# Expert stage of a convolution and attention hybrid: other group steps, two routing products, half precision pairs

## The reference

```python
def _L1_ffn_ref(x, router_w, router_b, expert_w, expert_b):
    B, N, D, C, E, K = (8, 8192, 128, 128, 8, 2)
    router_probs = jax.nn.softmax(x @ router_w + router_b, axis=-1)
    top_p, top_i = jax.lax.top_k(router_probs, K)
    top_p = top_p / jnp.sum(top_p, axis=-1, keepdims=True)
    expert_out = jnp.einsum('bnd,edc->bnec', x, expert_w) + expert_b
    gathered = jnp.take_along_axis(expert_out, top_i[..., None], axis=2)
    return jnp.einsum('bnk,bnkc->bnc', top_p, gathered)

t = t + _L1_ffn_ref(_ln_t(t), ...)      # residual, _ln_t is a layer norm per token
```

## Time and profile before

| | us |
|---|---|
| median of 3 runs | 2772.21 (2766.97 to 2772.77) |
| the profiled execution, its own time | 2768.08 |
| its span in the profile | 2766.2 |
| start of the expert stage in it | 2392.07 |
| first `scaled`, first `scaled_halves` (tile 0) | 2425.17, 2426.4 |
| last `scaled_halves` (tile 127) | 2760.47 |

### The profile page before, as it was taken

One profiled execution on the slowest core, in us unless ns is written; L12 is line 12 of the kernel. 1 busy time (PEld: TensorE's weight loads), 2 busy tenths in 40 slices (PEclk: granted clock), 3 DMA queues, 4 the chain that ended last, 5 costly groups with the idle time before them and its releaser, 6 DMA issues. The chain is left out here.

```text
span 2766.2 us, 33616 instructions
## 1 busy us (share of the span) xinstructions
PE 2267.1 (82%) x10862; PEld 1298.3 (47%) x10862; DVE 2087.2 (75%) x3702; ACT 1668.3 (60%) x2322; POOL 563.4 (20%) x693
## 2 busy tenths in 40 slices
PE   0594646759860599999999999999999999778877
PEld 0581213657630344444444444444444444466665
DVE  5327879756598778888888888888888888655566
ACT  0113012642237378888888888888888888556655
POOL 0002240002106502201221022101200000036567
PEclk9997866555565699999999999999999999779989
DMA  4600213000004000000000000000000000000001
GB/s 149 221 22 1 121 37 85 0 8 1 1 1 121 5 1 1 1 1 1 1 1 1 1 1 1 1 1 1 1 1 1 1 1 1 8 12 27 24 23 39
DMA packets 81022, 64.09 MB, mean 23 GB/s; under 512 B 11475, under 2 KB 78931, under 8 KB 79332
## 3 DMA queue, kind: packets, MB, share of 16 engines
q1 hardware_dynamic: 73604, 60.21, 6.6%
q10 hardware_dynamic: 7264, 1.94, 0.4%
HBM read 36.91 MB, written 25.17 MB: 22 GB/s over the span
## 5 line engine op out<-in xcount | busy, mean ns | idle before, releaser
L1751 ACT ACTIVATE inner<-banks,key_bias,scales 128x1024 f32<-128x1024 f32 x512 | 616.9, 1205 | 211.4 <-PE banks L1624 206.3
L1873 DVE TENSOR_TENSOR weights_low<-weights,weights_high 128x1024 f16<-128x1024 f32 x512 | 675.3, 1319 | 17.0
L1758 ACT ACTIVATE weights<-inner 128x1024 f32<-128x1024 f32 x512 | 541.1, 1057 | 16.1 <-DVE weights_low L1873 0.3
L1869 DVE CAST weights_high<-weights 128x1024 f16<-128x1024 f32 x512 | 371.0, 725 | 180.7 <-ACT weights L1758 167.6
L1624 PE MATMUL banks<-queries_high,keys_high 128*128 128x512 f16 x1024 | 304.6, 379 | 0.7 <-ACT inner L1751 0.7
L1639 PE MATMUL banks<-weights_high,tokens_low 128*128 128x512 f16 x1024 | 304.6, 379 | 0.0
L1624 PE MATMUL banks<-queries_low,keys_high 128*128 128x512 f16 x1024 | 304.6, 379 | 0.0
L1639 PE MATMUL banks<-weights_low,tokens_high 128*128 128x512 f16 x1024 | 304.6, 379 | 0.0
L1624 PE MATMUL banks<-queries_high,keys_low 128*128 128x512 f16 x1024 | 304.6, 379 | 0.0
L1639 PE MATMUL banks<-weights_high,tokens_high 128*128 128x512 f16 x1024 | 304.5, 379 | 0.0
L1947 POOL CAST sums_high<-sums 128x512 f16<-128x512 f32 x32 | 39.4, 1231 | 1089.6 <-ACT sums L1741 1071.7
(11 more groups left out here) (439 smaller groups left out, 3863.8 us busy)
## 6 DMA issues: line engine op xcount, KB each, us to landing
images_a<-in_x SPq DMA_DIRECT2D x4, 2048.0 KB, 16.8
tokens_scratch<-images_a SPq DMA_DIRECT2D x4, 2048.0 KB, 13.1
images_b<-tokens_scratch SPq DMA_DIRECT2D x32, 256.0 KB, 2.8
mixed_scratch<-images_a SPq DMA_DIRECT2D x4, 2048.0 KB, 13.1
spare<-in_x SPq DMA_DIRECT2D x32, 256.0 KB, 2.8
result<-group_result SPq DMA_DIRECT2D x32, 256.0 KB, 2.3
images_b<-mixed_scratch SPq DMA_DIRECT2D x10, 768.0 KB, 5.0
table<-tables ACTq DMA_DIRECT2D x1, 805.5 KB, 14.6
```

The costliest lines, as they stand in the source:

```text
L1751: act.activation(m.inner[:, t % 2, :], m.pair[t % 2], ACT.Exp, scale=m.fs[:, 1:2], bias=m.kb[:, c // QN % 2, k:k + 1]).then_inc(s.inner, 1)
L1758: act.activation(m.wt[:, t % 2, :], m.inner[:, t % 2, :], ACT.Exp).then_inc(s.outer, 1)
L1869: vec.tensor_copy(m.wH[:, t % DEEP, :], m.wt[:, t % 2, :]).then_inc(s.high, 1)
L1873: vec.tensor_tensor(m.wL[:, t % DEEP, :], m.wt[:, t % 2, :], m.wH[:, t % DEEP, :], ALU.subtract)\
```

## The change

`stage_ffn`, its plan and its buffers are changed, and nothing else:

- Types: tokens and weights are split into pairs of float16 instead of float32r. To fit the range, the weights are divided by a size (root of the sum of squares of all weights) and multiplied by 2^15. This is computed at the stage's start: a reduction of squares on DVE, one matmul with ones on PE, a floor on DVE, a root on ACT, a reciprocal and two scalings on DVE. The logits are multiplied back (`down`), and the gates' divisor gets `up`.
- Routing: `w8H` has eight more columns, the low parts of the routing weights, so the high tokens meet 16 columns in one matmul and the low tokens 8 in another. Eight matmuls for each group replace twelve. DVE adds the two halves where it copied the logits before. The logits of all batches use one place in PSUM, with a new wait (`copied`) at a batch's first group.
- Order: `normed` stands behind `scaled`, two tiles in the round of `prep` and two in the round after; `m.ln` has four buffers. `turn` and `high` stand two rounds later, `low` three, `logit` five (`DELAY`).
- Plan: batches of 3, 5, 8, 8, 8 groups. Groups begin in rounds 0, 0, 1, 1, 2, then 12 to 19 one in each, then 32, 34, 36, 39, 41, 43, 46, 48, and the same plus 32. The pieces of `algebra` stand in rounds 9 and 10 (four steps each), then from 27, 57 and 89 in four rounds with two steps each, where seven rounds had one step each.

```diff
-        m.w8H = sb(l2, "expert_weights_high", [P, EXPERTS * D + EXPERTS], F32R)[:, :]
-        m.w8L = sb(l2, "expert_weights_low", [P, EXPERTS * D + EXPERTS], F32R)[:, :]
-        m.ln = sb(l2, "normed", [P, 2, GRP, D])
-        m.lnH = sb(l2, "normed_high", [P, RING, GRP, P], F32R)
-        m.lnL = sb(l2, "normed_low", [P, RING, GRP, P], F32R)
+        m.w8H = sb(l2, "expert_weights_high", [P, EXPERTS * D + 2 * EXPERTS], F16)[:, :]
+        m.w8L = sb(l2, "expert_weights_low", [P, EXPERTS * D], F16)[:, :]
+        m.ln = sb(l2, "normed", [P, 4, GRP, D])
+        m.lnH = sb(l2, "normed_high", [P, RING, GRP, P], F16)
+        m.lnL = sb(l2, "normed_low", [P, RING, GRP, P], F16)
...
-BATCHES = [4, 8, 8, 8, 4]
-SETTLE = 11
+BATCHES = [3, 5, 8, 8, 8]
+DELAY = 5
...
         at, slots = first[k - 1] * GRP, BATCHES[k - 1] * GRP
+        parts = min(7, slots // 5)
+        spread = slots - 1 - parts - DELAY - 1
         for i in range(BATCHES[k]):
-            prep.setdefault(at + i * (slots - SETTLE) // BATCHES[k], []).append(first[k] + i)
-        for i in range(7):
-            pieces[at + slots - 8 + i] = k
-        exps[at + slots - 6] = k
+            prep.setdefault(at + i * spread // BATCHES[k], []).append(first[k] + i)
+        for i in range(parts):
+            pieces[at + slots - 1 - parts + i] = (k, parts)
+        exps[at + slots - parts] = k
...
-                reached(pe, s.gates, k - 1)
+                if t == first[k]:
+                    reached(pe, s.copied, k)
                 for j in range(GRP):
...
                     pe.matmul(part, m.lnH[:, t % RING, j, :], m.w8H[:, cols], start=True, stop=False)
-                    pe.matmul(part, m.lnH[:, t % RING, j, :], m.w8L[:, cols], start=False, stop=False)
-                    mm = pe.matmul(part, m.lnL[:, t % RING, j, :], m.w8H[:, cols], start=False, stop=True)
+                    mm = pe.matmul(part[:, 0:EXPERTS], m.lnL[:, t % RING, j, :], m.w8H[:, cols][:, 0:EXPERTS],
+                                   start=False, stop=True)
...
+            turn(0)
+            pe.wait_ge(s.cleared, 2)
+            pe.wait_ge(s.squared, 1)
+            pe.matmul(m.ps[7][:, 0:1], m.full, m.wsize[:, 0:1], start=True, stop=True).then_inc(s.summed, 1)
+            turn(1)
             for t in range(BATCHES[0]):
-                turn(t)
-                if t >= 1:
-                    logit(t - 1)
-            logit(BATCHES[0] - 1)
+                if t >= 2:
+                    turn(t)
+                logit(t)
             for n in range(NI):
                 expert(n)
+                for t in prep.get(n - DELAY, []):
+                    logit(t)
                 for t in prep.get(n - 2, []):
-                    logit(t)
-                for t in prep.get(n, []):
                     turn(t)
...
             for n in range(NI):
-                for t in prep.get(n, []):
-                    normed(t)
                 scaled(n)
                 for t in prep.get(n - 1, []):
+                    normed(t, (2, 3))
+                for t in prep.get(n - 2, []):
                     high(t)
+                for t in prep.get(n, []):
+                    normed(t, (0, 1))
...
-                c.step(vec.tensor_copy(logit, logits(k)))
+                wide = logits(k)
+                c.step(vec.tensor_scalar(logit, wide[:, :, 0], down, None, ALU.mult))
+                vec.scalar_tensor_tensor(out=logit, in0=wide[:, :, 1], scalar=down, in1=logit, op0=ALU.mult, op1=ALU.add)\
+                    .then_inc(s.copied, 1)
+                vec.wait_ge(s.copied, k + 1)
...
+                c.step(vec.tensor_scalar(total, total, up, None, ALU.mult))
...
-            c.step(vec.tensor_copy(m.w8H, m.w8))
-            vec.tensor_tensor(m.w8L, m.w8, m.w8H, ALU.subtract).then_inc(s.weights, 1)
-            for t in range(BATCHES[0]):
+            vec.tensor_tensor_reduce(square, m.w8, m.w8, 1.0, 0.0, ALU.mult, ALU.add, m.wsize[:, 0:1]).then_inc(s.squared, 1)
+            vec.wait_ge(s.summed, 1)
+            vec.tensor_scalar(m.wsize[:, 1:2], m.ps[7][:, 0:1], 1e-30, None, ALU.max).then_inc(s.floored, 1)
+            low(0)
+            vec.wait_ge(s.sized, 1)
+            c.step(vec.reciprocal(m.wsize[:, 3:4], m.wsize[:, 2:3]))
+            vec.tensor_scalar(down, m.wsize[:, 2:3], 2.0 ** -15, None, ALU.mult)
+            c.step(vec.tensor_scalar(up, m.wsize[:, 3:4], 2.0 ** 15, None, ALU.mult))
+            c.step(vec.tensor_scalar(m.w8H[:, 0:EXPERTS * D + EXPERTS], m.w8, up, None, ALU.mult))
+            vec.scalar_tensor_tensor(out=m.w8H[:, EXPERTS * D + EXPERTS:], in0=m.w8[:, EXPERTS * D:], scalar=up,
+                                     in1=m.w8H[:, EXPERTS * D:EXPERTS * D + EXPERTS], op0=ALU.mult, op1=ALU.subtract)\
+                .then_inc(s.weights, 1)
+            vec.scalar_tensor_tensor(out=m.w8L, in0=m.w8[:, 0:EXPERTS * D], scalar=up, in1=m.w8H[:, 0:EXPERTS * D],
+                                     op0=ALU.mult, op1=ALU.subtract).then_inc(s.weights, 1)
+            for t in range(1, BATCHES[0]):
                 low(t)
...
                 if n in pieces:
-                    work = work or algebra(pieces[n])
-                    next(work, None)
+                    k, parts = pieces[n]
+                    work = work or algebra(k)
+                    for _ in range(-(-8 // parts)):
+                        next(work, None)
...
-                for t in prep.get(n - 1, []):
+                for t in prep.get(n - 3, []):
                     low(t)
```

More of the change, by code:

```diff
@@ L311, in memory @@
         m.rank = sb(l2, "first_ranks", [P, EXPERTS])[:, :]
+        m.full = sb(l2, "ones_for_sums", [P, P])[:, :]
+        m.wsize = sb(l2, "weight_sizes", [P, 8])
     return m
@@ L1990, in batch_plan @@
         at, slots = first[k - 1] * GRP, BATCHES[k - 1] * GRP
+        parts = min(7, slots // 5)
+        spread = slots - 1 - parts - DELAY - 1
         for i in range(BATCHES[k]):
[L1992 to L1995 removed]
+            prep.setdefault(at + i * spread // BATCHES[k], []).append(first[k] + i)
+        for i in range(parts):
+            pieces[at + slots - 1 - parts + i] = (k, parts)
+        exps[at + slots - parts] = k
     return first, prep, pieces, exps
 def stage_ffn(nc, held, m, ins, out):
[L2002 removed]
+    s = semaphores(nc, held, "ffn", "loaded cleared biased v factor rooted weights ones normed turned high low logits shifted exp copied gates squared summed floored sized "
                    "tile_d tile_a chain scaled halved paired result stored0 stored1")
@@ L2090, in _, with normed @@
         def _(act):
-            def normed(t):
-                reached(act, s.turned, t - 1)
-                if t < 2:
+            def normed(t, tiles):
+                reached(act, s.turned, t - 3)
+                if t < 4:
                     act.wait_ge(s.ones, 1)
-                for j in range(GRP):
+                for j in tiles:
                     img = t * GRP + j
-                    e = act.activation(m.ln[:, t % 2, j, 0:D - 1], m.b[:, img, 0:D - 1], ACT.Identity,
+                    e = act.activation(m.ln[:, t % 4, j, 0:D - 1], m.b[:, img, 0:D - 1], ACT.Identity,
                                        scale=m.fac[:, 1, img:img + 1], bias=m.fac[:, 2, img:img + 1])
-                e.then_inc(s.normed, 1)
+                if tiles[-1] == GRP - 1:
+                    e.then_inc(s.normed, 1)
             def high(t):
@@ L2125, in _ @@
             for t in range(BATCHES[0]):
-                normed(t)
+                normed(t, range(GRP))
                 if t >= 1:
                     high(t - 1)
+                if t == 1:
+                    act.wait_ge(s.floored, 1)
+                    act.activation(m.wsize[:, 2:3], m.wsize[:, 1:2], ACT.Sqrt).then_inc(s.sized, 1)
             high(BATCHES[0] - 1)
```

20 lines of the change are left out of this document (10 added, 10 removed).

## The result

| | before | after |
|---|---|---|
| median, us | 2771.09 (4 runs, 2766.97 to 2772.77) | 2709.32 (4 runs, 2705.52 to 2712.36) |
| ratio, 95% interval | | 0.9779 (0.9762 to 0.9796) |
| profiled execution, its span | 2768.08, 2766.2 | 2705.52, 2703.7 |
| first `scaled`, first `scaled_halves` | 2425.17, 2426.4 | 2419.68, 2420.90 |
| last `scaled_halves` | 2760.47 | 2697.92 |

The change takes 62 us away. The windows of the changed kernel's last stage show where it ends up. Each runs from the start of `scaled_halves` of one tile to that of another (0, 12, 32, 64, 96, 127); the columns are those of the earlier trace rows.

What follows compares the result with a forecast made beforehand. Bound by engines waiting for each other, PE's list the chain with a hole. Terms from 2422 sum to 2708, plus 10 is span 2718, 48 less than 2766.2; 2772 - 48 = 2724 us, range 2700 to 2755.

Steps and rivals of the forecast that it cites:

- the allowance: 10 us added to the summed list for what it doesn't show: rounds at the lower clock and new small holes.
- tiles 0 to 8: Loop's first tiles, five groups begun: 24 us with PE at full clock from round 5, 31 if never; 28 taken.
- tiles 12 to 31: Eight group rounds 26.2, five quiet 7.7, four with a table 18.2, one 1.5: together 53.6 us.
- Rival 2: The lists run clean, no allowance, first tiles warm: 2710 us, or 2705 with ACT evening out its rounds; chance 0.13.
- The hole: PE's 1.03 us wait before a logit for `low`, with all experts behind it; claimed to go with the new order.
- The third of three rounds: Where groups are three rounds apart: 1.9 us, from `turn` 0.35, an expert 1.29 and about 0.25 of latencies.
- Types worth nothing in quiet rounds: Half precision cuts PE's tile from 1.40 to about 1.29 us, worth nothing in quiet rounds under POOL's 1.54.
- Logits: A group's eight routing matmuls on PE cost 0.5 to 0.9 us, 0.5 taken, where twelve cost 1.36.
- Gate tables: DVE's table in four rounds: 15.0 us, with four tiles 19.2, less about 1 for buffered tiles: 18.2.
- POOL's floor: POOL's 1.54 us a tile, untouched by the change, bounds all rounds without side work.
- Rival 3: TensorE at 1.2 GHz for most of the loop, a tile then 2.58 us: time 2812; chance 0.04.
- Its signs of being wrong: Long waits of `turn` for `normed`, granted clock under 0.8 in the last three batches, or changed price of `high` or `low`.

Runs made afterwards that it cites:

- the lighter PE: Changed kernel without the experts' product of low weights and high tokens, four matmuls a tile instead of six: 2709.8 us, 0.9776.
- put back alone: Changed kernel with a group's logits three rounds after its start instead of five: 2725.67 us, 0.9845 of the kernel before.
- the order alone: Kernel before with the new order, plan and buffers, keeping float32r pairs and twelve logit matmuls a group: 2732.34 us against 2769.04, 0.987.
- the lighter POOL: Changed kernel with POOL's middle addition left out and four `scaled_halves` buffers instead of two: 2695.71 us, 0.9722 of the kernel before.
- the first spread tables: Changed kernel with groups begun earlier, gate tables cut into single operations over 7, 20 and 28 rounds, ring of 32 groups: 2674.81 us, 0.9649.
- the maximum in PSUM: Changed kernel with the row maximum of a gate table written to PSUM, leaving the subtraction one SBUF input: 2707.77 us, 0.9761.

## Why the prediction was right, and where its steps were off

Its list, without the allowance, against the trace:

| | predicted | measured |
|---|---|---|
| first `scaled`, first `scaled_halves` | 2420.9, 2422 | 2419.68, 2420.90 |
| tiles 0 to 8 | 28 | 22.9 |
| tiles 9 to 11 | 13.5 | 14.2 |
| tiles 12 to 31 | 53.6 | 53.5 |
| tiles 32 to 63 | 68.8 | 70.0 |
| tiles 64 to 95 | 68.8 | 69.7 |
| from tile 96 to the last | 47.7 | 46.8 |
| the end | 5.7 | 5.8 |
| sum | 2708 | 2703.7 |

The direction and the mechanism held, and the median fell inside the range, 15 below the predicted time: 62 us gained for 48 forecast. The forecast had 0.62 of the chances and the rival whose number came 0.13, so the range was right because it took in that rival. By its steps:

- *Allowance.* The mis-sized term: 10 us for rounds at the lower clock and new small holes, where the list was already 4 too long. Rival 2 (2705 to 2710) is what came. New holes and rounds at the lower clock did come (3.24 instead of 0.65 in one subtraction, PE at 1.2 GHz behind waits at each table), and were paid by terms that were too high elsewhere, the first tiles above all. That the sum is off by only 4 is in part luck.
- *Tiles 0 to 8.* 28 was put between 24, for a PE at full clock from round 5 on, and 31; 22.9 was measured. PE was at full clock one round sooner: the granted clock was 0.69 in the first 10.9 us and 1.00 in the 12.0 behind them (the 0.79 up to tile 12 takes in the table's pause too). With the lighter PE, at 1.2 GHz for 8 us more, the same tiles took 24.8. What else was too long in the side by side lists wasn't tested.
- *The hole.* It went (2.8 us of waits for `low` in the whole stage, had 1.03 for one), and put back alone it cost 16 us. ACT is next late, as said: rounds of 2.24 and 1.77 against 2.25 and 1.79.
- *The third of three rounds.* Put at 1.9, it took 2.15, and 1.72 with the lighter PE: the path through `turn` and an expert was right, its 0.25 of latencies too small (0.51 is left in either case). Nineteen rounds took 37.6 instead of 36.7, and most of that is this term.
- *Types worth nothing in quiet rounds.* True: 1.51 there, by POOL. But they are worth more in group rounds than the text suggests: without them the order gives 37 instead of 62. The prediction's own figures held this (1.40 + 1.36 + 0.35 in a round with a group is 3.1), and it never summed the order alone.
- *Logits.* Eight matmuls took 0.20, not 0.5. The nearest row (130 columns, 0.06) was too far away; it changed nothing, since PE isn't last.
- *Gate tables.* DVE's four rounds last 17.9 (2556.37 to 2574.27), where the sum had 19.2 and took off 1 for buffered tiles. Less four tiles of 1.04 that leaves 13.7 for the table, not 15.0, and DVE is the bound there as said. The 1 us taken off has no ground: 14.3 + 7.3 against 20.5 compares seven tiles with six, and the difference is the seventh. The two errors nearly cancel. In the fourth table the long subtraction comes on top.
- *POOL's floor.* 1.51 instead of 1.54: 0.9 us less in the last 31 tiles. Why is not known.
- *Rival 3.* Its first half is real: a lighter PE gets the lower clock (0.59 in the first tiles), as the sentence on the Trainium skill in the prediction had it. Its price came only in the first tiles, 2 us; elsewhere PE wasn't last.
- *Tiles 12 to 31.* 53.6 listed, 53.5 measured, with the dense group rounds at 3.03, ACT's 1.01 + 2.01. The stretch gains only 0.7, since the plan moved work into it.
- *Its signs of being wrong.* One of them shows: `turn` waits for `normed`, 22.2 us in 25 waits, where the prediction thought the step a round old. It costs nothing where ACT is gapless, so the sign was badly chosen. The granted clock of the last three windows was 0.93, 0.93 and 1.00, and `low` kept its price (683 ns for 689).

## What to carry to other kernels

In a loop of engines with fixed lists, sum each engine's list for every kind of round and take the largest; that gave this loop's 277 us to 3 us (with the first nine tiles 5 too long and the large batches 2 too short), and an allowance on top made it worse. A step whose input passes through two other engines belongs several rounds behind its start (16 us for two rounds). When one kind of round is bound by DVE and another by POOL or ACT, cut the side work into single operations and lay it under the rounds that another engine bounds: that gave 34 us more than the change (9 of them by earlier groups alone, and cutting finer without moving gave nothing that can be told), and it was to be read from the windows, in which no engine was busy throughout.

## What the runs showed of the hardware that was not expected

- Half precision matmuls of 8 and 16 columns, each with weights of its own, start 0.025 us apart at the full clock; those of 8 columns in float32r took 0.113.
- A DVE operation that needs two SBUF inputs, or a copy from SBUF to SBUF, can be held beside an unbroken POOL for 2.8 to 4.7 us instead of 0.3 to 0.84, until POOL has a gap. In 13 cases in ten kernels it ended 0.15 to 0.29 us behind POOL's last operation. There was none in the kernel before, whose POOL waits for ACT more (167.7 us), and none in the kernels with the order alone, the lighter POOL and the first spread tables. The kernel with the lighter PE had three, at 3.23 or 3.24 each.
- PE stood at 1.2 GHz behind a wait of 3.44 us as behind 6.39, with two tiles of 2.6 each. The kernel with the maximum in PSUM has such a stretch at its third table's end and took 2.4 us more than the changed kernel for tiles 32 to 64 (72.4 and 70.0), with a median that is no different. So one window that differs by 2 us doesn't show what an edit did.
